# The chain of matrix exponentials moves from a stage of its own into the first attention: the Taylor rounds into its fill, the squarings and products into its drain

## The chip, the cores and the metric

One Trainium2 chip, one of its cores. The metric is the device time of one execution in microseconds (us). Engines: TensorE (PE), VectorE (DVE), ScalarE (ACT), GpSimd (POOL) and SyncE (SP), which issues most transfers.

## The reference

Four layers, each a cross-attention and a feed-forward, on x of 16 x 256 tokens by 128, with 64 context rows per batch. What matters here is in layer 0:

```python
x = x + xattn0(layernorm(x), ctx)            # 16 heads, key mask
# layer 0's feed-forward, on xn = layernorm(...)
moe      = sum over 6 experts of weight * (gelu(xn @ ew1[e] + eb1[e]) @ ew2[e] + eb2[e])
for i in range(4):
    moe  = moe @ expm(gens[i])               # gens: 4 matrices of 128 x 128
abel     = gelu(xn @ aw1 + ab1) @ aw2 + ab2
x        = x + residual + gated mix of abel and moe
```

The four rotations depend on weights alone, so the kernel computes R = expm(g0) expm(g1) expm(g2) expm(g3) once and folds it into the down weights: W2R = ew2 R, b2R = eb2 R. Each exponential is a Taylor polynomial of degree 8 of the matrix scaled by 2^-6, and six squarings.

## The kernel before

The program is a row of stages; a stage ends at a barrier of all engines. The first ones are `load`, `prep_mha` (keys and values), `mha(core, 0, key_mask=True)` (the first attention), `fold_rotations` (the exponentials) and `ffn_moe_rotated`. The feed-forward needs X and its statistics MV from the attention, and W2R, b2R, up_h and up_l from `fold_rotations`.

**The attention** is a software pipeline written out by hand: every engine runs a loop over slots t = -8 to 43 (FIRST = -8, LAST = T + 12, T = 32 tiles of 128 tokens), and an engine's order within a slot is the order of the `if`s in its loop. Slots -8 to -1 are the fill, 32 to 43 the drain. On PE a slot has scores (t), scores_T (t-5), shifts, heads_T (t-10), attend (t-7), tokens (t-9), x_transposes and queries (for four tiles at once, in slots -7, -6 and -3, -2 of the fill, then every four slots) and output (t-10). On DVE: bn_stats and bn_aggr of the second half of x (`arrive`, slots -7, -6, -5 and -3), reciprocal and at (t-10), X (t-11), largest (t), statistics, and q_low after each `queries`. On ACT: attended, normalise, heads_T (the copy aT), exponentials (t-5), shifts, and the copies xT and qh. Queries go out to memory and come back stacked (`write_queries`, `read_queries` on SP) before scores may read them. POOL builds keys(b) (L605), a memset of a part of qs for the first three batches (L632) and add_bo(b) (L609), as far ahead as its buffers go.

**The chain** (`fold_rotations`) works on two halves of two matrices each. A Taylor round: PE multiplies A1T by E (L1085, 4 matmuls), DVE adds A1 from PSUM into tmp (L1124) and scales tmp into the next E (L1125, from SBUF to SBUF); seven rounds, then a transpose (L1090) and its copy (L1128). A squaring: PE makes E E and its transpose (L1097, L1098, 8 matmuls), DVE adds twice the old (L1136, L1137); in the sixth it also adds the identity (L1140, L1141). Then three products (L1103, L1105, L1108) with copies, and the fold (L1111, L1112: 13 matmuls), copied out by L1151 and L1152. A matmul of 32-bit data shows as two entries in the trace. ACT and POOL meanwhile make up_h (L1067) and up_l (L1072). Steps wait on each other by the semaphores s_pe, s_dve, s_r and s_rp.

All weights of later stages, and the mask of the last attention (raw3, 1 MB), are loaded by `load_later` on SP during `prep_mha`.

Of the kernel before, what the change touches and what calls it, by code (L numbers as in the profile page):

```python
# [316 lines left out]

def mha(core, L, mask=None, key_mask=False, gather=False):
# [13 lines left out]
    with Stage(core, f"mha{L}") as st:  # L332
# [95 lines left out]
        def _(pe):  # L428
# [95 lines left out]
        def _(act):  # L524
# [50 lines left out]
            for t in range(FIRST, LAST):  # L575
# [14 lines left out]
                if t % QT == 2 and live(t + 6):  # L590
                    q_evac(quad(t + 6))

        @blk.gpsimd
        def _(pool):
# [32 lines left out]
            else:  # L627
                for b in range(B):
                    keys(b)
                    if key_mask and b < QB:  # L630
                        pool.wait_ge(s["k"], b + 1)
                        pool.memset(qs[b][3 * HR:K0, :, :].bitcast(F32), 1.0).then_inc(s["one"], 1)  # L632
                        pool.wait_ge(s["one"], b + 1)
                    add_bo(b)

        @blk.vector
        def _(dve):
            def pipeline(masked):
# [44 lines left out]
                for t in range(FIRST, LAST):  # L683
# [355 lines left out]
TAYLOR = 8  # L1039
SQUARINGS = 6  # L1040


def fold_rotations(core):


    w = lambda n: core.w("rot", n)
    ident = core.w("ctx", "ident")
    N4 = NROT * P
    with Stage(core, "rot") as st:
        A1, A1T = st.sb("A1", [P, N4]), st.sb("A1T", [P, N4])  # L1050
        E = [st.sb(f"E{u}", [P, N4]) for u in range(2)]
        ET = [st.sb(f"ET{u}", [P, N4]) for u in range(2)]
        tmp, R = st.sb("tmp", [P, N4]), st.sb("R", [P, P])
        MT, M34 = st.sb("MT", [P, P]), st.sb("M34", [P, P])

        pE, pF = ([st.ps(f"p{n}{h}", [P, 512]) for h in range(2)] for n in "EF")
        pW = st.ps("pW", [P, 3, 512])
        pB = st.ps("pB", [P, 512])
        s_pe, s_dve, s_own = ([st.sem(f"{n}{h}") for h in range(2)] for n in ("pe", "dve", "own"))
        s_r, s_rp, s_high = st.sem("r"), st.sem("rp"), st.sem("high")  # L1060
        blk = st.block()
        g = lambda t, n: t[:, P * n:P * n + P]


        @blk.scalar
        def _(act):
            act.activation(core.up_h[:], w("up"), ACT.Copy).then_inc(s_high, 1)  # L1067

        @blk.gpsimd
        def _(pool):  # L1070
            pool.wait_ge(s_high, 1)
            pool.tensor_tensor(core.up_l[:], w("up"), core.up_h[:], ALU.subtract)  # L1072

        W = 2 * P
        half = lambda t, h: t[:, W * h:W * h + W]
        U = (TAYLOR - 1) % 2
        V, VT = (U + SQUARINGS) % 2, SQUARINGS % 2

        @blk.tensor
        def _(pe):  # L1080
            for step in range(TAYLOR - 1):
                for h in range(2):
                    pe.wait_ge(s_dve[h], step + 1)
                    for n in range(2):
                        ins = pe.matmul(g(pE[h], n), g(A1T, 2 * h + n), g(E[step % 2], 2 * h + n), start=True, stop=True)  # L1085
                    ins.then_inc(s_pe[h], 1)
            for h in range(2):
                pe.wait_ge(s_dve[h], TAYLOR)
                for n in range(2):
                    ins = pe.transpose(g(pF[h], n), g(E[U], 2 * h + n), ident)  # L1090
                ins.then_inc(s_pe[h], 1)
            for k in range(SQUARINGS):
                for h in range(2):
                    pe.wait_ge(s_dve[h], TAYLOR + 1 + k)
                    for n in range(2):
                        e, t = g(E[(U + k) % 2], 2 * h + n), g(ET[k % 2], 2 * h + n)
                        pe.matmul(g(pE[h], n), t, e, start=True, stop=True)  # L1097
                        ins = pe.matmul(g(pF[h], n), e, t, start=True, stop=True)  # L1098
                    ins.then_inc(s_pe[h], 1)
            for h in range(2):  # L1100
                pe.wait_ge(s_dve[h], TAYLOR + 1 + SQUARINGS)
                if h == 0:
                    ins = pe.matmul(g(pE[0], 0), g(E[V], 1), g(ET[VT], 0), start=True, stop=True)  # L1103
                else:
                    ins = pe.matmul(g(pE[1], 0), g(ET[VT], 2), g(E[V], 3), start=True, stop=True)  # L1105
                ins.then_inc(s_pe[h], 1)
            pe.wait_ge(s_r, 1)
            pe.matmul(g(pF[0], 0), MT[:], M34[:], start=True, stop=True).then_inc(s_rp, 1)  # L1108
            pe.wait_ge(s_r, 2)
            for c in range(2 * NE):  # L1110
                pe.matmul(pW[:, c // 4, P * (c % 4):P * (c % 4) + P], w("ew2T")[:, P * c:P * c + P], R[:], start=True, stop=True)  # L1111
            pe.matmul(pB[0:NE, 0:P], w("eb2T"), R[:], start=True, stop=True).then_inc(s_rp, 1)  # L1112

        @blk.vector
        def _(dve):
            link = [Chain(dve, s_own[h]) for h in range(2)]
            for h in range(2):
                dve.tensor_scalar(half(A1T, h), half(w("gensT"), h), 2.0 ** -SQUARINGS, None, ALU.mult)
                link[h](dve.tensor_scalar(half(A1, h), half(w("gens"), h), 2.0 ** -SQUARINGS, None, ALU.mult))
                dve.tensor_scalar(half(E[0], h), half(A1, h), 1.0 / TAYLOR, None, ALU.mult).then_inc(s_dve[h], 1)  # L1120
            for step in range(1, TAYLOR):
                for h in range(2):
                    dve.wait_ge(s_pe[h], step)
                    link[h](dve.tensor_tensor(half(tmp, h), pE[h][:, 0:W], half(A1, h), ALU.add))  # L1124
                    dve.tensor_scalar(half(E[step % 2], h), half(tmp, h), 1.0 / (TAYLOR - step), None, ALU.mult).then_inc(s_dve[h], 1)  # L1125
            for h in range(2):
                dve.wait_ge(s_pe[h], TAYLOR)
                dve.tensor_copy(half(ET[0], h), pF[h][:, 0:W]).then_inc(s_dve[h], 1)  # L1128
            i2 = ident.unsqueeze(1).to_broadcast([P, 2, P])
            m2 = lambda t, h: half(t, h).rearrange("p (n d) -> p n d", n=2)  # L1130
            for k in range(SQUARINGS):
                for h in range(2):
                    last = k == SQUARINGS - 1
                    dve.wait_ge(s_pe[h], TAYLOR + 1 + k)
                    dve.wait_ge(s_dve[h], TAYLOR + 1 + k)
# [1449 lines left out]
```

## Time and profile before

| | |
|---|---|
| three runs, us | 1602.37, 1605.2, 1614.73 (median 1605.2) |
| the profiled execution, us | 1620.42, of which 1618.6 are its span |
| mean granted clock of PE in it | 0.828 |
| busy share: PE, DVE, ACT, POOL | 75%, 63%, 38%, 16% |

```profile
## 2 busy tenths in 40 slices
PE   3688769999967655241935885999999999658852
DVE  7577736666647885962337775455566655546768
PEclk9699769999985555565965897999999999968985
```

A slice is 40.5 us; the digits are the busy share in tenths, and PEclk the granted clock of PE in tenths of its full one. In the rows further below, "stretches" give each engine's busy time with its number of instructions, and the timeline gives start, duration, engine, line, operation, output<-inputs, and in brackets the idle time before it with what ended it; PEld is PE's loading of weights. The first attention lies in slices 1 to 4 (31.7 to 170.3 us), the stage of the exponentials in the end of slice 4 and the start of slice 5 (170.6 to 213.7 us), where PE's digit falls.

### The profile page before, as it was taken

What the parts mean: (1) busy time and instruction counts of PE and PEld (TensorE: products, weight loads), DVE (VectorE), ACT (ScalarE), POOL (GpSimd) and SP (SyncE); (2) the same over time, 40 slices, a digit from 0 to 9 for tenths busy, and PEclk for the clock granted to TensorE, in tenths of its full rate; (3) what the DMA queues carried; (4) which work ended last, traced back from release to release, by engine and by line L of the source; (5) the groups of instructions that cost most, each with busy time, mean ns of one, the idle gap of its engine ahead of it and who ended that gap; (6) DMA issues with size and microseconds to landing.
All of it is one profiled execution on the core that took longest, in us unless ns stands there. A gap on an engine that the chain in (4) does not pass through costs nothing. (4 is left out here: it accounts for less than half of the span.)

```text
span 1618.6 us, 22585 instructions
## 1 busy us (share of the span) xinstructions
PE 1213.5 (75%) x6805; PEld 883.7 (55%) x6805; DVE 1012.8 (63%) x3435; ACT 610.2 (38%) x1143; POOL 256.6 (16%) x240
## 2 busy tenths in 40 slices
PE   3688769999967655241935885999999999658852
PEld 1455659898954434210723653677777777425531
DVE  7577736666647885962337775455566655546768
ACT  3565024444433222110223652344443444336641
POOL 1331000010001100043356330000000000023402
PEclk9699769999985555565965897999999999968985
DMA  8441000000000022042215320000000000024301
GB/s 254 127 118 43 1 1 1 1 1 0 1 1 1 0 85 87 1 129 67 87 41 146 95 77 3 0 1 0 1 1 0 0 1 1 1 65 119 99 6 52
DMA packets 57700, 69.43 MB, mean 43 GB/s; under 512 B 10880, under 2 KB 38784, under 8 KB 56960
## 3 DMA queue, kind: packets, MB, share of 16 engines
q1 hardware_dynamic: 54272, 61.78, 13.3%
q0 software_dynamic: 3328, 6.43, 1.3%
q8 instruction: 48, 0.79, 0.2%
q14 instruction: 52, 0.43, 0.1%
HBM read 44.99 MB, written 23.59 MB: 42 GB/s over the span
## 5 line engine op out<-in xcount | busy, mean ns | idle before, releaser
L605 POOL TENSOR_TENSOR mha_ks<-KS,w_ctx 104x1024 fp32r<-104x1024 f32 (+1 forms) x48 | 90.8, 1895 | 674.7 <-POOLq L99 500.0
L2173 DVE SCALAR_TENSOR_TENSOR tree_hl<-tree_pH,tree_hh 128x512 fp32r<-128x512 f32 x192 | 132.4, 690 | 94.5 <-ACT tree_hh L2070 92.5
L2070 ACT ACTIVATE tree_hh<-tree_pH 128x512 fp32r<-128x512 f32 x192 | 114.8, 598 | 146.0 <-PE tree_pH L1974 146.0
L654 DVE TENSOR_REDUCE mha_nm<-mha_pS 128x16 f32<-128x1024 f32 x96 | 117.2, 1221 | 27.4 <-PE mha_pS L449 27.3
L449 PE MATMUL mha_pS<-mha_ks,mha_qs 96*128 96x256 f32 (+1 forms) x384 | 82.6, 344 | 32.6 <-DVE mha_nm L654 18.1
L1323 ACT ACTIVATE ffn_hid<-ffn_pH,w_ffn 128x512 f32<-128x512 f32 x128 | 85.6, 689 | 54.7 <-PE ffn_pH L1248 54.1
L1987 PE MATMUL tree_pY<-tree_hh,w2h 128*128 128x512 f32 x192 | 100.9, 525 | 4.5 <-DVE tree_hl L2173 4.4
L560 ACT ACTIVATE XH<-mha_pST 128x1024 f32<-128x1024 f32 x96 | 98.0, 1021 | 11.8 <-PE mha_pST L470 11.6
L1432 DVE SCALAR_TENSOR_TENSOR ffn_acc<-ffn_pE,ffn_wt,ffn_acc 128x128 f32<-128x128 f32 x192 | 54.1, 346 | 71.3 <-PE ffn_pE L1261 71.3
L1261 PEld LDWEIGHTS ffn_pE<-W2R,ffn_hid 128*128 128x128 f32 x768 | 93.7, 192 | 4.4
L1261 PE MATMUL ffn_pE<-W2R,ffn_hid 128*128 128x128 f32 x768 | 93.9, 276 | 0.0
L449 PEld LDWEIGHTS mha_pS<-mha_ks,mha_qs 96*128 96x128 f32 (+1 forms) x384 | 61.3, 220 | 52.0 <-issue 29.8
L1971 PE MATMUL tree_pH<-tree_xTh,w1h 128*128 128x512 f32 x192 | 81.0, 422 | 1.0 <-DVE tree_sel L2167 1.0
L1973 PE MATMUL tree_pH<-tree_xTh,w1l 128*128 128x512 f32 x192 | 76.5, 398 | 0.0
L1972 PE MATMUL tree_pH<-tree_xTl,w1h 128*128 128x512 f32 x192 | 76.2, 397 | 0.0
L1987 PE MATMUL tree_pY<-tree_hl,w2h 128*128 128x512 f32 x192 | 76.2, 397 | 0.0
L1974 PE MATMUL tree_pH<-tree_sel,mix 128*128 128x512 bf16 x192 | 75.3, 392 | 0.0
L1987 PE MATMUL tree_pY<-tree_hh,w2l 128*128 128x512 f32 x192 | 75.2, 391 | 0.0
L470 PE MATMUL mha_pST<-mha_qs,mha_ks 104*128 104x256 f32 (+1 forms) x384 | 66.2, 297 | 1.9 <-ACT XH L560 0.7
L479 PE MATMUL mha_pO<-XH,VB 128*18 128x256 f32 x768 | 61.1, 390 | 0.0
L433 PE MATMUL mha_pQ<-w_ctx,mha_xh 128*128 128x128 f32 x96 | 20.7, 356 | 51.3 <-ACT mha_xh L535 44.8
L470 PEld LDWEIGHTS mha_pST<-mha_qs,mha_ks 104*128 104x128 f32 (+1 forms) x384 | 55.9, 201 | 4.1 <-ACT XH L560 2.9
(453 smaller groups left out, 2821.8 us busy)
## 6 DMA issues: line engine op xcount, KB each, us to landing
mha_qs<-queries SPq DMA_DIRECT2D x72, 256.0 KB, 4.1
queries<-mha_qh SPq DMA_DIRECT2D x24, 256.0 KB, 2.1
queries<-mha_ql SPq DMA_DIRECT2D x24, 256.0 KB, 2.4
EW<-in_L_W_dram SPq DMA_DIRECT2D x32, 128.0 KB, 2.7
EW<-in_tree_full_dram SPq DMA_DIRECT2D x2, 1536.0 KB, 8.0
slots_in<-route_zero SPq DMA_DIRECT2D x4, 640.0 KB, 10.9
w_rot<-in_rot_dram SPq DMA_DIRECT2D x1, 2307.0 KB, 8.5
X<-in_x_dram SPq DMA_DIRECT2D x8, 256.0 KB, 8.0
```

The costliest lines, as they stand in the source:

```text
L449: ins = pe.matmul(pS[:, NH * g:NH * g + NH, :], qs[u][0:KC, g, c0:c0 + P], ks[b % KB][0:KC, g, :, :], start=True, stop=True)
L470: ins = pe.matmul(pST[:, n, :], ks[b % KB][0:K1, g, h0:h0 + 2, :], qs[u][0:K1, g, c0:c0 + S], start=True, stop=True)
L560: act.activation(PT[b % PB][:, CU * i:CU * i + CU, :], pST[:], ACT.Exp, scale=SC).then_inc(s["P"], 1)
L605: pool.tensor_tensor(ks[b % KB][0:K1, :, :, :], kb, hb, ALU.mult).then_inc(s["k"], 1)
L654: dve.tensor_reduce(nm[:, t, :], pS[:], AX.X, ALU.max, negate=True).then_inc(s["nm"], 1)
L1261: ins = pe.matmul(pE[p % 2][:, j, :], hc, core.W2R[:, P * r:P * r + P], start=(c == 0), stop=(c == 1))
L1323: act.activation(hid[p % 2][:, c, :], pH[c][:], ACT.Gelu, bias=b).then_inc(s["h"], 1)
L1971: pe.matmul(pH[k % 2][:], core.w1h[:, k0], xTh[u][:], start=True, stop=False)
L1973: pe.matmul(pH[k % 2][:], core.w1l[:, k0], xTh[u][:], start=False, stop=False)
L1987: ins = pe.matmul(bank[:], w2[:, k0], h[k % 2][:], start=(c == 0 and i == 0), stop=False)
L2070: act.activation(hh[k % 2][:], pH[k % 2][:], ACT.Relu).then_inc(s["h"], 1)
L2173: dve.scalar_tensor_tensor(hl[k % 2][:], pH[k % 2][:], 0.0, hh[k % 2][:], ALU.max, ALU.subtract).then_inc(s["lo"], 1)
```

## The change

`fold_rotations` is gone. A class `Rotations` has the same steps, numbered k: 0 scales the generators, 1 to 7 are Taylor rounds, 8 the transpose, 9 to 14 the squarings, 15 and 16 the products, 17 the fold. `mha` calls step 0 on DVE ahead of its slots, step k = t + 9 in the fill (t = -8 to -1) and k = t - 23 in the drain (t = 32 to 40). On PE a step stands behind scores and ahead of all else in its slot; on DVE it is last in its slot. Up_h and up_l move to ACT's slot 34 and the end of POOL's work.

The chain has no buffers of its own: E and ET lie in raw3, A1, A1T and tmp in W2R, R and the products in the generators' place; the PSUM is pST in the fill and pS in the drain (the fold also pQ and pST). So the load of raw3 moves from `load_later` into the feed-forward's stage as one transfer, and the generators become a pack of their own (512 KB), loaded on SP between the two halves of x.

```diff
+            rot_at = {t: t + 9 for t in range(-8, 0)}
+            rot_at.update({t: t - T + 9 for t in range(T, T + 9)})
...
                 if live(t):
                     scores(t)
+                if rot and t == UN:
+                    for h in range(2):
+                        pe.wait_ge(rot.s_dve[h], rot.RISING + 1)
+                if t in rot_at:
+                    if t == T:
+                        pe.wait_ge(s["nm"], T)
+                    if rot_at[t] == rot.LAST:
+                        pe.wait_ge(s["P"], TB * B)
+                        pe.wait_ge(s["q"], NG)
+                        pe.wait_ge(core.loaded, 16 * core.loads)
+                    rot.on_tensor(pe, rot_at[t])
                 if live(t - UN):
...
+                if rot and t == T + 2:
+                    act.wait_ge(core.loaded, 16 * core.loads)
+                    act.activation(core.up_h[:], core.w("rot", "up"), ACT.Copy).then_inc(rot.s_high, 1)
...
                     if live(t - HT - 1):
                         dve.wait_ge(s["bn"], x + 1)
                         dve.bn_aggr(MV[:, x, :], bn[x % 2][:])
+                    if t in rot_at:
+                        rot.on_vector(dve, rot_link, rot_at[t])
...
+        @blk.sync
+        def _(sp):
+            sp.dma_start(core.raw3[:], tiles(core.A["mask3"])).then_inc(core.mask3_loaded, 16)
+            sp.wait_ge(core.mask3_loaded, 16)
...
-    for q in range(2):
-        half = slice(T // 2 * q, T // 2 * q + T // 2)
-        later(core.raw3[:, half, :], tiles(A["mask3"])[:, half, :])
...
+                if q == NG // 2 - 1:
+                    sp.dma_start(core.pack["rotg"][:], A["rotg"]).then_inc(core.generators_loaded, 16)
...
-                fold_rotations(core)
```

How PE and DVE take a step in the new code (inside `Rotations`, for each half h, beside the squarings and products, which have the old form):

```diff
+            pe.wait_ge(self.s_dve[h], k)
+            if k < TAYLOR:
+                for n in range(2):
+                    ins = pe.matmul(g(pE, n), g(self.A1T, 2 * h + n), g(E[(k - 1) % 2], 2 * h + n), start=True, stop=True)
...
+            dve.wait_ge(self.s_pe[h], k)
+            if k < TAYLOR:
+                link[h](dve.tensor_tensor(half(self.tmp, h), pE, half(self.A1, h), ALU.add))
+                dve.tensor_scalar(half(E[k % 2], h), half(self.tmp, h), 1.0 / (TAYLOR - k), None, ALU.mult).then_inc(self.s_dve[h], 1)
```

Three places in the engines' order. The first is PE's start of the first attention, before (L433 x_transposes, L438 queries, L449 scores) and after (L555, L560, L571 are the same; L371 a Taylor round of 4 matmuls, L374 the transpose):

```order
L433 MATMUL mha_pQ<-w_ctx,mha_xh 128x128 x4
L438 MATMUL mha_pQ<-mha_xT,w_mha 128x512
L433 MATMUL mha_pQ<-w_ctx,mha_xh 128x128 x4
L438 MATMUL mha_pQ<-mha_xT,w_mha 128x512
L449 MATMUL mha_pS<-mha_ks,mha_qs 128x256 x8
```

```order
L371 MATMUL mha_pST<-raw,W2R 128x128 x8
L555 MATMUL mha_pQ<-w_ctx,mha_xh 128x128 x4
L371 MATMUL mha_pST<-raw,W2R 128x128 x4
L560 MATMUL mha_pQ<-mha_xT,w_mha 128x512
L371 MATMUL mha_pST<-raw,W2R 128x128 x12
L555 MATMUL mha_pQ<-w_ctx,mha_xh 128x128 x4
L371 MATMUL mha_pST<-raw,W2R 128x128 x4
L560 MATMUL mha_pQ<-mha_xT,w_mha 128x512
L374 MATMUL mha_pST<-w_ctx,raw 128x128 x4
L571 MATMUL mha_pS<-mha_ks,mha_qs 128x256 x8
```

Two rounds now stand ahead of the first x_transposes, a third ahead of the first queries, six ahead of the second x_transposes, seven ahead of the second queries, and the whole rising half of the chain ahead of the first scores.

The second is DVE at the same place, after (L872 and L876 statistics of x, L783 q_low, L413 and L414 a half of a round); before, the same rows stood there without L413 and L414:

```order
L413 TENSOR_TENSOR W2R<-mha_pST,W2R 128x256
L414 TENSOR_SCALAR raw<-W2R 128x256
L872 BN_STATS mha_gbn<-X 128x6 x4
L876 BN_AGGR MV<-mha_gbn 128x2 x4
L783 SCALAR_TENSOR_TENSOR mha_ql<-mha_pQ,w_mha,mha_qh 128x512
L413 TENSOR_TENSOR W2R<-mha_pST,W2R 128x256
L414 TENSOR_SCALAR raw<-W2R 128x256
L413 TENSOR_TENSOR W2R<-mha_pST,W2R 128x256
L414 TENSOR_SCALAR raw<-W2R 128x256
```

The third round's adds stand behind q_low, which waits for the queries, which on PE stand behind the third round's matmuls.

The third is DVE in the drain, before (L691 to L716, five operations a slot) and after, in slots 37 and 38, with the sixth squaring between them:

```order
L697 TENSOR_TENSOR mha_at<-mha_pA,mha_rc 128x128
L704 TENSOR_TENSOR X<-mha_pY,X 128x128
L709 BN_STATS mha_bn<-X 128x6
L716 BN_AGGR MV<-mha_bn 128x2
L691 RECIPROCAL mha_rc<-mha_pA 128x16
L697 TENSOR_TENSOR mha_at<-mha_pA,mha_rc 128x128
```

```order
L855 BN_AGGR MV<-mha_bn 128x2
L420 SCALAR_TENSOR_TENSOR raw<-raw,mha_pS 128x256
L421 SCALAR_TENSOR_TENSOR raw<-raw,mha_pS 128x256
L424 TENSOR_TENSOR raw<-raw,w_ctx 128x256
L425 TENSOR_TENSOR raw<-raw,w_ctx 128x256
L420 SCALAR_TENSOR_TENSOR raw<-raw,mha_pS 128x256
L421 SCALAR_TENSOR_TENSOR raw<-raw,mha_pS 128x256
L424 TENSOR_TENSOR raw<-raw,w_ctx 128x256
L425 TENSOR_TENSOR raw<-raw,w_ctx 128x256
L830 RECIPROCAL mha_rc<-mha_pA 128x16
L836 TENSOR_TENSOR mha_at<-mha_pA,mha_rc 128x128
```

Between the statistics of one tile and the reciprocal of the next now stand eight operations of the chain.

## Rows read from the trace of the kernel before

**Rows 1.** Stretches: length; busy PE, PEld, DVE, ACT, POOL; PEclk; DMA share, GB/s.

```profile
37.00:44.00 7.00, 3.39 (x7) 1.45 (x8) 2.93 (x17) 3.67 (x9) 6.64 (x5) 0.50 0.00 0
44.00:51.50 7.50, 2.96 (x6) 0.98 (x5) 2.59 (x15) 2.82 (x6) 5.02 (x5) 0.50 0.79 223
147.50:159.60 12.10, 10.31 (x88) 6.27 (x87) 6.74 (x30) 7.67 (x15) 0.00 (x0) 1.00 0.03 7
159.60:170.60 11.00, 6.60 (x39) 3.74 (x39) 6.34 (x27) 2.10 (x8) 0.00 (x0) 0.79 0.00 0
170.60:182.80 12.20, 8.28 (x32) 7.13 (x32) 9.46 (x20) 1.91 (x1) 3.81 (x1) 0.50 0.01 2
182.80:188.60 5.80, 5.12 (x29) 3.67 (x28) 5.23 (x15) 0.00 (x0) 0.00 (x0) 0.97 0.00 0
188.60:202.00 13.40, 12.39 (x98) 11.18 (x96) 10.26 (x26) 0.00 (x0) 0.00 (x0) 1.00 0.01 1
```

**Rows 2.** Timeline (start us, us, engine, line): the stage of the exponentials, its ends.

```profile
170.12 0.18 DVE L716 BATCH_NORM_AGGREGATE MV<-mha_bn 128x2 f32<-128x6 f32 x1
...
170.60 1.92 ACT L1067 ACTIVATE up_h<-w_rot 128x2048 fp32r<-128x2048 f32 x1 [2.01 <-PEq L99]
...
213.44 0.27 DVE L1152 COPY b2R<-rot_pB 6x128 f32<-6x128 f32 x1
```

**Rows 3.** Timeline: a GpSimd operation and DVE's beside it, at three places.

```profile
33.90 1.80 POOL L632 MEMSET mha_qs<- 3x2048 f32 x1
...
34.86 0.87 DVE L746 TENSOR_SCALAR mha_nt<-mha_nt 128x16 f32<-128x16 f32 x1
...
37.81 1.89 POOL L605 TENSOR_TENSOR mha_ks<-KS,w_ctx 107x1024 fp32r<-107x1024 f32 x1
...
172.59 3.81 POOL L1072 TENSOR_TENSOR up_l<-w_rot,up_h 128x2048 fp32r<-128x2048 f32 x1 [32.80 <-ACTq L99]
...
173.22 3.33 DVE L1125 TENSOR_SCALAR rot_E<-rot_tmp 128x256 f32<-128x256 f32 x1
...
176.91 0.29 DVE L1125 TENSOR_SCALAR rot_E<-rot_tmp 128x256 f32<-128x256 f32 x1
```

**Rows 4.** Timeline: the fill, from the scales to the first scores.

```profile
35.98 0.17 DVE L748 SCALAR_TENSOR_TENSOR mha_NB<-MV,RS 128x16 f32<-128x16 f32 x1
...
36.97 0.38 DVE L735 BATCH_NORM_AGGREGATE MV<-mha_gbn 128x2 f32<-128x6 f32 x4
...
37.98 1.09 PE L433 MATMUL mha_pQ<-w_ctx,mha_xh 128*128 128x128 f32 x4 [7.74 <-ACT mha_xh L535]
...
39.76 2.07 PE L438 MATMUL mha_pQ<-mha_xT,w_mha 128*128 128x512 f32 x2 [0.69 <-ACT mha_xT L540]
...
42.67 0.75 DVE L644 SCALAR_TENSOR_TENSOR mha_ql<-mha_pQ,w_mha,mha_qh 128x512 fp32r<-128x512 f32 x1 [4.00 <-ACT mha_qh L545]
...
48.52 0.64 POOL L609 TENSOR_TENSOR X<-X,w_mha 128x256 f32<-128x256 f32 x1
...
51.55 1.19 PE L449 MATMUL mha_pS<-mha_ks,mha_qs 99*128 99x256 f32 x4 [3.91 <-issue]
```

**Rows 5.** Timeline: the chain's own steps, from a round to the fold.

```profile
178.67 1.78 PEld L1085 LDWEIGHTS rot_pE<-rot_E,rot_A1T 128*128 128x128 f32 x8 [0.28 <-DVE rot_E L1125]
...
180.74 1.78 PEld L1085 LDWEIGHTS rot_pE<-rot_E,rot_A1T 128*128 128x128 f32 x8 [0.28 <-DVE rot_E L1125]
...
203.56 0.42 DVE L1141 TENSOR_TENSOR rot_ET<-rot_ET,w_ctx 128x256 f32<-128x256 f32 x1
...
206.46 4.63 PEld L1111 LDWEIGHTS rot_pW<-rot_R,w_rot 128*128 128x128 f32 x24 [0.68 <-DVE rot_R L1148]
...
211.64 1.89 DVE L1151 COPY W2R<-rot_pW 128x512 f32<-128x512 f32 x3 [5.23 <-PE rot_pB L1112]
```

**Rows 6.** Timeline: the drain, scores_T (L470), heads_T (L492), statistics (L716).

```profile
152.79 0.54 PEld L470 LDWEIGHTS mha_pST<-mha_qs,mha_ks 107*128 107x128 f32 x4 [0.32 <-ACT XH L560]
...
159.66 0.33 PE L492 MATMUL mha_pA<-w_ctx,mha_at 128*128 128x128 f32 x1 [0.52 <-DVE mha_at L697]
...
160.16 0.18 DVE L716 BATCH_NORM_AGGREGATE MV<-mha_bn 128x2 f32<-128x6 f32 x1
...
161.66 0.33 PE L492 MATMUL mha_pA<-w_ctx,mha_at 128*128 128x128 f32 x1 [0.52 <-DVE mha_at L697]
```

More of the change, by code:

```diff
@@ L381, in mha @@
         LD, LM, LW = 16 * 3, 16, 16 * 2
+        if key_mask:
+            rot = Rotations(core, st, pST[:].rearrange("p c s -> p (c s)"), pS[:].rearrange("p h k -> p (h k)"),
+                            pQ[:], pST[:].rearrange("p c s -> p (c s)")[:, 0:512])
+            rot_at = {t: t + 9 for t in range(-8, 0)}
+            rot_at.update({t: t - T + 9 for t in range(T, T + 9)})
+        else:
+            rot, rot_at = None, {}
         blk = st.block()
@@ L505, in _ @@
                     scores(t)
+                if rot and t == UN:
+                    for h in range(2):
+                        pe.wait_ge(rot.s_dve[h], rot.RISING + 1)
[7 more added lines that the diff above has]
+                    rot.on_tensor(pe, rot_at[t])
                 if live(t - UN):
@@ L634, in _ @@
                     add_bo(b)
+            if rot:
+                pool.wait_ge(rot.s_high, 1)
+                pool.tensor_tensor(core.up_l[:], core.w("rot", "up"), core.up_h[:], ALU.subtract)
         @blk.vector
@@ L753, in _ @@
             scales(0)
+            if rot:
+                rot_link = [Chain(dve, rot.s_own[h]) for h in range(2)]
+                rot.on_vector(dve, rot_link, 0)
             if gather:
@@ L1038 @@
 NROT, NE, EH = 4, 6, 256
[L1039 to L1135, printed above, removed]
-                    link[h](dve.scalar_tensor_tensor(half(E[(U + k + 1) % 2], h), half(E[(U + k) % 2], h), 2.0, pE[h][:, 0:W], ALU.mult, ALU.add))
-                    ins = dve.scalar_tensor_tensor(half(ET[(k + 1) % 2], h), half(ET[k % 2], h), 2.0, pF[h][:, 0:W], ALU.mult, ALU.add)
-                    if last:
-                        link[h](ins)
-                        link[h](dve.tensor_tensor(m2(E[V], h), m2(E[V], h), i2, ALU.add))
-                        ins = dve.tensor_tensor(m2(ET[VT], h), m2(ET[VT], h), i2, ALU.add)
-                    ins.then_inc(s_dve[h], 1)
-            dve.wait_ge(s_pe[0], TAYLOR + SQUARINGS + 1)
-            link[0](dve.tensor_copy(MT[:], g(pE[0], 0)))
-            dve.wait_ge(s_pe[1], TAYLOR + SQUARINGS + 1)
-            dve.tensor_copy(M34[:], g(pE[1], 0)).then_inc(s_r, 1)
-            dve.wait_ge(s_rp, 1)
-            dve.tensor_copy(R[:], g(pF[0], 0)).then_inc(s_r, 1)
-            dve.wait_ge(s_rp, 2)
-            for n in range(3):
-                dve.tensor_copy(core.W2R[:, 512 * n:512 * n + 512], pW[:, n, :])
-            dve.tensor_copy(core.b2R[:], pB[0:NE, 0:P])
@@ L2430, in four_layers @@
             with ExitStack() as early:
-                place(core, early, ["mha0", "rot"])
+                place(core, early, ["mha0", "rotg", "rot"])
                 core.itok = sb(early, "itok", [P, B * SK], I32)
@@ L2504, in packs @@
     A = lambda k: np.asarray(I[n + k])
-    out["rot"] = [("gens", A("gens").transpose(1, 0, 2).reshape(P, -1)), ("gensT", A("gens").transpose(2, 0, 1).reshape(P, -1)),
-                  ("ew2T", A("ew2").reshape(-1, P).T), ("eb2T", A("eb2").T),
+    out["rotg"] = [("gens", A("gens").transpose(1, 0, 2).reshape(P, -1)), ("gensT", A("gens").transpose(2, 0, 1).reshape(P, -1))]
+    out["rot"] = [("ew2T", A("ew2").reshape(-1, P).T), ("eb2T", A("eb2").T),
                   ("up", np.concatenate([A("ew1").transpose(1, 0, 2).reshape(P, -1), A("aw1")], 1))]
```

97 lines of the change are left out of this document (added).

## The prediction

> **What bounds the kernel now.** I read the busy time by stretch first [rows 1], since the page's shares are averages over stages. The stage that goes, from the last statistics of the attention at 170.30 us (170.12 + 0.18) to its last copy at 213.71 (213.44 + 0.27), takes 43.4 us in which nothing else runs [rows 2]. It is a chain of PE and DVE handing each other one matrix: in the timeline PE waits for DVE and DVE for PE [rows 5]. So what it gives back, if the work costs nothing elsewhere, is 43.4 us. What it costs elsewhere depends on what the fill and the drain are made of. In the fill PE is busy for 3.39 of 7.0 and 2.96 of 7.5 us, at a granted clock of 0.50, the lower level of 1.2 GHz [rows 1]. That looks like room, but it is a chain too: scales, x_transposes, queries, q_low, memory and back, scores [rows 4]. In the drain PE is busy for 10.31 of 12.1 us up to 159.6, at 1.00, so there is next to no room in slots 32 to 36, and 6.60 of 11.0 us afterwards [rows 1]. POOL is busy for 6.64 of 7.0 us in the first part of the fill and idle in the drain.
>
> **The fill, step by step.** Each round takes 2.07 us with both halves under way at PE's lower clock (178.67 to 180.74) [rows 5]; PE's part is 4 passes of a half in 1.05 us, and 0.1 to 0.2 us pass to the next engine. The scaling operation of DVE, from SBUF to SBUF, is the thing to look at. Alone it took 0.29 us; started at 173.22 beside POOL's up_l it took 3.33 and ended at 176.55, just behind POOL's end at 176.40. So did a smaller one beside a memset: 34.86 + 0.87 = 35.73, POOL's end 35.70 [rows 3]. In the fill POOL works without a break on keys (1.89 us), memset (1.80) and add_bo (0.64) until it has done all it may, at 49.16 before [rows 3, 4]. So each of the first scalings waits for the end of a POOL operation, and two of them a round do so in turn.
>
> From the scales' end at 36.15 [rows 4]: step 0 is six operations, done at 38.2. Round 1: PE's half 0 at 38.2, half 1 at 39.4; the scalings end with keys(1) at 40.2 and with the second memset at 42.1. Round 2 on PE ends at 43.3, and only then come the first x_transposes, 5.3 us later than before (37.98). On DVE a pass of statistics takes 1.3 us (it ended 36.97 + 0.38 = 37.35, behind the scales' end) [rows 4], and round 2's scalings end with keys(2) and the third memset at 44.9 and 46.8. Round 3 on PE ends at 48.0, then queries (before 39.76, so +8.2), and q_low ends 3.66 us behind its start (39.76 to 43.42), at 51.7. Before, 8.1 us of memory traffic followed (43.42 to 51.55) and set the first scores. Now these run beside the rest of the chain, which lasts longer: round 3 on DVE until 54.9 (keys(3) and add_bo stand in its way), statistics 1.3, round 4 until 57.7, round 5 60.0, statistics again, round 6 62.8; on PE x_transposes and round 7 until 64.3; queries to q_low 3.66, until 68.0; round 7 on DVE 69.5; the transpose 70.0; first scores. Against 51.55 that is 18.5 us. PE is busy almost without a gap from 57 on; in the old stage its clock rose from 0.50 to 0.97 in the stretch behind a like one, 8.28 busy of 12.2 us [rows 1], so I take 1.0 us off for the second queries: **+17.5**. Everything behind the first scores shifts by that: the four later tiles' queries are back before their scores want them, and SP, ACT and POOL have nothing else to be late with. What is late next is nothing new.
>
> The ends for the fill: if scalings did not wait for POOL, the same list gives 13.6, 12.6 with the clock; if also the six of step 0 and the rest waited, 20.5. I take the row, since the operation is the same one, of the same size, beside the same engine.
>
> **The drain.** A squaring is 16 passes, 11.18 / 6 = 1.86 us of weight loads at full clock [rows 1]. PE has it ahead of scores_T in slots 32 to 36, where it idled for some 0.3 us a slot waiting for the exponentials (0.32 at 152.79) [rows 6]: 5 x (1.86 - 0.3) and a little more in slot 32, **+8.1**. DVE has some 1.3 us of its own in a slot (27 operations in 6.34 us [rows 1], five a slot, and gaps) and now four of 0.42 (203.56 [rows 5]), 1.8 with gaps, which fits into a PE slot of 3.6. In slot 37 the sixth squaring has eight such operations, 3.5 us with gaps, which start behind the statistics (160.34 + 8.1 = 168.4) and end at 171.9; the next tile's heads_T, before at 161.66 [rows 6], needs DVE's reciprocal and product first and comes at 172.6: +10.9 so far, **+2.8** for this. Steps 15 and 16 are three small copies and three matmuls, hidden but for **0.2** in a loop of 2.0 us between PE, DVE and ACT (159.66 to 161.66). The fold is 13 matmuls, 26 passes, 5.2 us (206.46 to 211.64), then copies of 2.07 us (211.64 to 213.71) [rows 2, 5]; of these 7.3, 2.4 lie beside the loop of the tiles 30 and 31: **+4.9**. I take the lower clock for the fold, since before it fell at the end of the drain (0.79 over its last stretch [rows 1]); at the full one it is 2.2 less. Up_h is 1.92 us on ACT [rows 2], which is busy for 7.67 us of five and a half slots [rows 1], 1.4 of now 3.6 each: **+0.4**; up_l is on an idle POOL, and no DVE operation of the drain at that time is a scaling. Together **+16.4**; low end 13.4 (fold at full clock, nothing for up_h, no loss in the sixth squaring's hand-over), high end 18.
>
> **The rest at nothing.** The mask's load now runs in the feed-forward's stage, where SP has nothing and the data is wanted four stages later. The generators' load stands on SP's queue ahead of the second half of x, which is first read at 36 us. The stage's barrier (0.3 us) is the same one fewer on both sides of my sum's ends.
>
> **The sum.** 43.4 - 17.5 - 16.4 = 9.5 us less. On the profiled execution, 1620.4 us, that gives 1610.9. This execution stands 15.2 us above the median of the three runs, and the difference carries over: 1605.2 - 9.5 = **1595.7**. Best and worst of the bounds: 43.4 - 12.6 - 13.4 = 17.4 and 43.4 - 20.5 - 18 = 4.9 less, so 1588 to 1600; the three runs lie 2.8 below and 9.5 above their median, which widens it to **1585 to 1604**.
>
> **Rivals.**
> 1. *The fill hides its part.* If the memory traffic behind q_low went on setting the first scores, the delay would be that of the first q_low alone, 8.2 us or, without waits on POOL, 4.8. Then the saving is 43.4 - 16.4 - 8.2 = 18.8 and up to 22: 1583 to 1586. For it speaks that the fill's PE is half idle. Against it: rounds 4 to 7 follow one another behind q_low in both queues, and 5 rounds of 2 us and two passes of statistics are more than 8.1. 10%.
> 2. *PE falls to its lower clock in the drain* (the case on the other side). Its place is slots 32 to 37: PE now waits for DVE at each step. At 1.2 GHz six squarings cost 11.2 us more and the attention's own matmuls of five slots, about 1.7 us each, 8.5 more: 43.4 - 17.5 - 36.1, a loss of 10: 1615. It decides against the change once half of this comes. Against it: before, PE kept 1.00 through 159.6 at 10.31 busy of 12.1 us, and kept it into the sparser part; the new slots are denser. By the Trainium skill, "TensorE: Matmul & The Clock Gate", section "HAM oscillation — how this bites in real kernels", short bursts of matmuls with waits between them bring the array back to half its clock again and again. If that page's rule held for the handing to and fro in these slots, the time would be this rival's; the rows of the drain before do not show it. 6%.
> 3. *DVE and POOL block each other more than counted*, also POOL for DVE, so that keys(3) and later keys come late and the first slots stall: another 5 us, a saving of 4.5: 1600.7. Within my range. 12%.
> 4. *The start of the first slots gets the full clock* after the dense fill (before 0.50): five slots at 0.4 us each, saving 11.5: 1593.7, within my range too.
>
> **Chances.** The forecast with rivals 3 and 4 has 80%, rival 1 10%, rival 2 6%, the rest 4%. Measurement of this kernel tells about 1%, 16 us, from no change. Faster by over 1%, below 1589.2, needs a saving of 16: rival 1, and the better end of mine, together 22%. Slower by over 1%, above 1621: 3%. Within 1%: 75%.
>
> **What would show it.** Right: first scores at about 69 us, first x_transposes at 43; several scalings (L414) of 1 to 2 us which end with a POOL operation; slots of the drain 3.6 us apart; the sixth squaring's eight DVE operations just ahead of a reciprocal, and PE idle there; the end of the attention at some 204 us, against 213.7 of the old stage. Wrong: first scores near 60 (rival 1), a granted clock below 0.9 in the first part of the drain (rival 2), or scalings of 0.29 us throughout.

## The result, and the profile after

| | before | after |
|---|---|---|
| median of 6 runs each, us | 1607.52 (1602.37 to 1614.73) | 1594.61 (1591.95 to 1597.61) |
| ratio, 95% interval | | 0.9919 (0.9892 to 0.9946) |
| the profiled execution, us | 1620.42 | 1597.43, of which 1595.6 are its span |
| mean granted clock of PE in it | 0.828 | 0.833 |

The change gives 12.9 us, between 8.7 and 17.4. The forecast was 1595.7 and the measurement 1594.6, but so close a hit is partly luck: the saving forecast was 9.5, and the median of before came out 2.3 us higher than in the three runs it was taken from.

The page of the changed kernel, its second part (slices of 39.9 us):

```profile
PE   4688879999957664244916885999999999658852
...
PEclk9699979999975555565955997999999999969985
```

Counted from slice 0, the first attention and the chain now end with slice 4, and PE's digits in slices 4 and 5, before 7 and 6, are 8 and 7.

Stretches of the changed kernel (length; busy PE, PEld, DVE, ACT, POOL; PEclk; DMA share, GB/s), in the form of [rows 1]: the drain with the squarings, a stretch behind them, the fold, the feed-forward's stage and the routing's:

```profile
161.70:185.50 23.80, 21.96 (x202) 17.85 (x200) 18.49 (x63) 10.18 (x17) 3.81 (x1) 1.00 0.02 6
...
188.50:190.00 1.50, 1.04 (x5) 0.91 (x5) 0.70 (x4) 0.28 (x1) 0.00 (x0) 0.50 0.00 0
190.00:193.50 3.50, 3.50 (x29) 3.16 (x27) 1.05 (x5) 0.00 (x0) 0.00 (x0) 0.90 0.00 0
...
198.30:454.20 255.90, 235.39 (x1600) 212.53 (x1601) 154.62 (x703) 108.07 (x173) 20.29 (x16) 0.95 0.02 5
454.20:739.30 285.10, 142.54 (x478) 94.89 (x478) 203.14 (x969) 64.27 (x124) 43.40 (x48) 0.54 0.14 47
```

The timeline of the changed kernel in the fill, to be read beside [rows 3] and [rows 4] (L889 is the last of the scales, L371 and L374 are PE's Taylor rounds and transpose, L413 and L414 DVE's add and scaling, L741 and L768 POOL's keys and memset, L783 q_low, L571 the first scores):

```profile
35.95 0.17 DVE L889 SCALAR_TENSOR_TENSOR mha_NB<-MV,RS 128x16 f32<-128x16 f32 x1
...
39.78 1.83 POOL L768 MEMSET mha_qs<- 3x2048 f32 x1
...
40.24 1.53 DVE L414 TENSOR_SCALAR raw<-W2R 128x256 f32<-128x256 f32 x1
...
42.84 1.06 PE L555 MATMUL mha_pQ<-w_ctx,mha_xh 128*128 128x128 f32 x4
...
47.30 1.91 PE L560 MATMUL mha_pQ<-mha_xT,w_mha 128*128 128x512 f32 x2
...
50.05 0.75 DVE L783 SCALAR_TENSOR_TENSOR mha_ql<-mha_pQ,w_mha,mha_qh 128x512 fp32r<-128x512 f32 x1 [2.63 <-ACT mha_qh L678]
...
51.05 1.89 POOL L741 TENSOR_TENSOR mha_ks<-KS,w_ctx 107x1024 fp32r<-107x1024 f32 x1
...
51.16 1.93 DVE L414 TENSOR_SCALAR raw<-W2R 128x256 f32<-128x256 f32 x1
...
53.46 0.30 DVE L414 TENSOR_SCALAR raw<-W2R 128x256 f32<-128x256 f32 x1
...
55.44 0.29 DVE L414 TENSOR_SCALAR raw<-W2R 128x256 f32<-128x256 f32 x1
...
61.90 1.02 PE L560 MATMUL mha_pQ<-mha_xT,w_mha 128*128 128x512 f32 x2
...
63.68 0.75 DVE L783 SCALAR_TENSOR_TENSOR mha_ql<-mha_pQ,w_mha,mha_qh 128x512 fp32r<-128x512 f32 x1 [2.39 <-ACT mha_qh L678]
...
66.00 0.71 PE L571 MATMUL mha_pS<-mha_ks,mha_qs 99*128 99x256 f32 x4
```

The scaling that starts at 40.24 ends at 41.77, right behind the memset's end at 41.61; the one at 51.16 ends at 53.09, behind the keys' end at 52.94. With no POOL operation beside it one takes 0.29 (at 55.44). The first scores come at 66.00, 14.45 us later than in [rows 4].

The same in the drain, beside [rows 6] (L379 the squarings, L614 heads_T, L384 the first of the products' steps, L359 the fold, L392 its copies, L855 statistics):

```profile
159.60 0.72 PE L571 MATMUL mha_pS<-mha_ks,mha_qs 99*128 99x256 f32 x4
...
173.63 0.39 PE L379 MATMUL mha_pS<-raw 128*128 128x128 f32 x2
...
177.26 0.39 PE L379 MATMUL mha_pS<-raw 128*128 128x128 f32 x2
...
179.53 0.27 PE L614 MATMUL mha_pA<-w_ctx,mha_at 128*128 128x128 f32 x1
...
185.61 0.49 PE L384 MATMUL mha_pS<-raw 128*128 128x128 f32 x2 [1.22 <-DVE raw L425]
186.18 0.33 PE L614 MATMUL mha_pA<-w_ctx,mha_at 128*128 128x128 f32 x1
...
190.01 2.28 PE L359 MATMUL mha_pS<-w_rotg,w_rot 128*128 128x128 f32 x16
...
193.54 1.29 DVE L392 COPY W2R<-mha_pS 128x512 f32<-128x512 f32 x2 [2.32 <-PE mha_pST L360]
...
196.22 0.33 PE L614 MATMUL mha_pA<-w_ctx,mha_at 128*128 128x128 f32 x1 [1.37 <-DVE mha_at L836]
...
198.10 0.18 DVE L855 BATCH_NORM_AGGREGATE MV<-mha_bn 128x2 f32<-128x6 f32 x1
```

The row of the kernel before that scores(31) is counted from:

```profile
145.05 0.72 PE L449 MATMUL mha_pS<-mha_ks,mha_qs 99*128 99x256 f32 x4
```

Slots are 3.6 us apart (173.63 to 177.26), and the attention ends at 198.28, where the old stage ended at 213.71 [rows 2]: 15.4 us earlier in the trace. It splits into 43.4 saved, 14.45 paid in the fill and 13.4 in the drain (scores(31), at 159.60, to the end took 38.68 us, before 25.25). Between the first scores and scores(31) nothing changed: 93.6 us, before 93.5.

### The profile page after: what moved, and what is told of

The parts are those of the page before. It is cut to its first block and busy times, and to the rows that moved or that the text cites. A ratio compares the mean times of both kernels' runs of the same rounds, so it can differ in the third digit from the quotient of the medians.

```text
span 1595.6 us, 22581 instructions
## 1 busy us (share of the span) xinstructions
PE 1206.2 (76%) x6805; PEld 880.0 (55%) x6805; DVE 1014.6 (64%) x3435; ACT 608.7 (38%) x1143; POOL 255.4 (16%) x240
## 3 DMA queue, kind: packets, MB, share of 16 engines
q1 hardware_dynamic: 51328, 61.78, 13.4%
## 5 line engine op out<-in xcount | busy, mean ns | idle before, releaser
L741 POOL TENSOR_TENSOR mha_ks<-KS,w_ctx 104x1024 fp32r<-104x1024 f32 (+1 forms) x48 | 90.8, 1894 | 686.8 <-POOLq L99 498.0
L2208 DVE SCALAR_TENSOR_TENSOR tree_hl<-tree_pH,tree_hh 128x512 fp32r<-128x512 f32 x192 | 132.3, 689 | 93.9 <-ACT tree_hh L2105 92.0
L571 PE MATMUL mha_pS<-mha_ks,mha_qs 96*128 96x256 f32 (+1 forms) x384 | 81.6, 340 | 25.9 <-DVE mha_nm L793 21.6
L1296 PE MATMUL ffn_pE<-W2R,ffn_hid 128*128 128x128 f32 x768 | 93.5, 275 | 0.0
L571 PEld LDWEIGHTS mha_pS<-mha_ks,mha_qs 96*128 96x128 f32 (+1 forms) x384 | 59.9, 215 | 44.0 <-issue 22.7
L1281 PE MATMUL ffn_pH<-ffn_xTh,up_h 128*128 128x512 f32 x128 | 57.2, 447 | 0.8 <-ACT ffn_hid L1358 0.5
```

The source lines that it names most:

```text
L571: ins = pe.matmul(pS[:, NH * g:NH * g + NH, :], qs[u][0:KC, g, c0:c0 + P], ks[b % KB][0:KC, g, :, :], start=True, stop=True)
L741: pool.tensor_tensor(ks[b % KB][0:K1, :, :, :], kb, hb, ALU.mult).then_inc(s["k"], 1)
L1296: ins = pe.matmul(pE[p % 2][:, j, :], hc, core.W2R[:, P * r:P * r + P], start=(c == 0), stop=(c == 1))
L2208: dve.scalar_tensor_tensor(hl[k % 2][:], pH[k % 2][:], 0.0, hh[k % 2][:], ALU.max, ALU.subtract).then_inc(s["lo"], 1)
```

## The experiments

Seven variants of the changed kernel were timed and profiled, and the kernel before was profiled a second time; all ratios are to the kernel before. The first attention does not start at the same time in every profile: the last of the scales starts at 35.95 us in the changed kernel's and between 35.16 and 35.84 in those of the variants without a stage ahead. Counted from there the four profiles with the same fill agree on the first scores within 0.02 us (30.04 to 30.06), so differences in the fill are best counted from there too.

**Fill alone, drain alone.** The two halves of the change, one at a time. In `fill_only` the rising half stays in the fill and the falling half has its own stage behind the attention; in `drain_only` the rising half has its own stage ahead of the attention. The cores of the two diffs:

```diff
             rot_at = {t: t + 9 for t in range(-8, 0)}
-            rot_at.update({t: t - T + 9 for t in range(T, T + 9)})
...
                 mha(core, 0, key_mask=True)
+                falling_stage(core)
```

```diff
-            rot_at = {t: t + 9 for t in range(-8, 0)}
-            rot_at.update({t: t - T + 9 for t in range(T, T + 9)})
+            rot_at = {t: t - T + 9 for t in range(T, T + 9)}
...
                 prep_mha(core, 0, True, statistics=True)
+                rising_stage(core)
```

> The Taylor rounds and the transpose stay in the fill of the first attention; the squarings, products and the fold go back into a stage of their own behind it, with up_h and up_l. My theory (fill and drain each cost what their own chains say, and add up): the first scores stay at 66 us, the drain is as in the kernel before, so the attention ends at about 185, and the stage takes 25 (before: 188.6 to 213.7). Less than before by 43.4 - 25.1 - 14.5 = 4 us, ratio 0.9975. The rival (the fill hides the rising half and the drain carries the whole cost) wants some 18 us less than before, ratio 0.989.

> The rising half (scaling, Taylor rounds, transpose) gets a stage of its own ahead of the first attention; the falling half stays in the drain. My theory: that stage takes 15 us (18 in the kernel before, of which 3 was one scaling waiting for POOL, which is idle here), the fill is as before (first scores 15.5 us behind the stage's start, so as late as now), the drain costs 13.4. Less than before by 43.4 - 15.3 - 13.4 = 14.7 us, ratio 0.991, the same as with the rounds in the fill: the fill's placement by itself gives nothing. The rival (the fill's room hides a good part of the rounds) wants this kernel to be 10 us slower than the changed one, ratio 0.997.

Measured: `fill_only` 1606.92 us, ratio 1.0007 (0.9990 to 1.0025); `drain_only` 1594.51, ratio 0.9920 (0.9898 to 0.9941), which is the changed kernel's own. The rival of `drain_only` (0.997) falls, and so does that of `fill_only` (0.989). The timeline of `drain_only`, where the chain's rounds are done before the first x_transposes (L572; L588 the scores):

```profile
52.42 1.09 PE L572 MATMUL mha_pQ<-w_ctx,mha_xh 128*128 128x128 f32 x4 [7.00 <-ACT mha_xh L685]
...
65.99 1.19 PE L588 MATMUL mha_pS<-mha_ks,mha_qs 99*128 99x256 f32 x4 [3.91 <-issue]
```

65.99 against 66.00: in the fill the rising half costs what it costs in a stage of its own ahead of it, and the placement in the fill gives nothing. Of the some 15.5 us in the trace, 11.7 are the falling half's (25.1 in the old stage, 13.4 in the drain). The other 3.8 are the rising half's, 18.3 in the old stage and 14.5 in either of the new places; 3.0 of them are the one scaling that up_l held up in the old stage (3.33 against 0.29 us [rows 3]). Starting up_l elsewhere in the kernel before would have shown whether these 3.0 can be had without moving anything; it wasn't tried.

`fill_only` was to bring 4 us, since the rising half had taken 18.3 in the old stage (170.3 to 188.6) and delays the first scores by 14.5. Its profile shows what took most of them back. Stretches, of the start of its falling stage and of the one ahead of it:

```profile
183.00:185.20 2.20, 0.80 (x2) 0.50 (x2) 0.94 (x4) 0.19 (x2) 0.00 (x0) 0.50 0.00 0
185.20:189.40 4.20, 3.79 (x18) 3.83 (x19) 0.84 (x2) 1.85 (x1) 2.27 (x1) 0.50 0.00 0
```

The stage takes 27.4 us where the same steps took 25.1 in the old stage (188.6 to 213.7). There the clock stood at 0.97 in the stretch ahead of the squarings [rows 1]; here it had already fallen at the sparse end of the drain (0.50 in the 2.2 us ahead of the stage, with PE busy for 0.80), and the squarings stay at 0.50 for the stage's first 4.2 us. By the starts of the rows, 1.3 of the 2.3 us lie in the squarings and products (19.1 us against 17.8), 0.7 in the fold up to its copies (5.85 against 5.18), and 0.3 ahead of the first squaring. The fold's part need not be the split's: its 24 entries took 4.83 us in the first profile of the kernel before and 5.46 in the second. The saving left in the trace is 1.1 us; the time shows none, and its interval allows up to 1.6.

**Do the scalings wait for POOL?** `tmp_psum` writes the round's sum back to PSUM in place, so that the scaling reads PSUM instead of SBUF; nothing else changes.

```diff
-                link[h](dve.tensor_tensor(half(self.tmp, h), pE, half(self.A1, h), ALU.add))
-                dve.tensor_scalar(half(E[k % 2], h), half(self.tmp, h), 1.0 / (TAYLOR - k), None, ALU.mult).then_inc(self.s_dve[h], 1)
+                link[h](dve.tensor_tensor(pE, pE, half(self.A1, h), ALU.add))
+                dve.tensor_scalar(half(E[k % 2], h), pE, 1.0 / (TAYLOR - k), None, ALU.mult).then_inc(self.s_dve[h], 1)
```

> The changed kernel with one edit: a round's sum is written back to PSUM in its place instead of to tmp in SBUF, so the scaling that follows reads PSUM. My theory (the scaling from SBUF to SBUF waits for POOL's operation): the scalings take 0.42 us each without exception, first scores 3 us earlier, at 63, and the attention ends at 195.3; ratio to before 0.990. The rival (DVE's waits are hidden behind queries and transposes anyway): scalings of 0.42 but first scores at 66 and no gain.

Measured: 1592.57 us, ratio 0.9920 (0.9903 to 0.9937). Its timeline:

```profile
36.99 1.94 POOL L741 TENSOR_TENSOR mha_ks<-KS,w_ctx 107x1024 fp32r<-107x1024 f32 x1
37.91 0.42 DVE L414 TENSOR_SCALAR raw<-mha_pST 128x256 f32<-128x256 f32 x1
...
60.61 1.20 PE L571 MATMUL mha_pS<-mha_ks,mha_qs 99*128 99x256 f32 x4
```

Every scaling takes 0.42, beside POOL or not, and the first scores come at 60.61, 5.4 us earlier; counted from the scales, which started at 35.16 here, it is 4.6. The five scalings that were held up in the changed kernel (1.17, 1.53, 0.89, 1.53 and 1.93 us) had lost 5.6 us over 0.29 each, and 14 scalings at 0.42 cost 1.8 more, which leaves 3.8; the first queries also took 1.02 us instead of 1.91. The theory of the lock is shown, and the rival (hidden waits) falls. The Trainium skill, "SBUF — State Buffer", section "Who interferes with whom", says that scalar-and-tensor operations of VectorE from SBUF may take ports that it shares with GpSimd, and that the later one then waits for the whole instruction: the pair of profiles agrees, 1.53 against 0.42. The attention's end came 4.2 us earlier in the trace, counted from the scales. The time does not show it: 2 us by the medians and nothing by the ratios (0.9920 against 0.9919, intervals of 3 to 5 thousandths), so how much of the 4.2 arrives is not settled by this run.

**Does the order in PE's queue set the fill's price?** `late_rounds` takes a slot's round behind its x_transposes and queries instead of ahead of them.

```diff
-                if t in rot_at:
+                if t in rot_at and t >= 0:
...
                     queries(quad(t + 6))
+                if t in rot_at and t < 0:
+                    rot.on_tensor(pe, rot_at[t])
```

> The changed kernel with one edit: in the fill PE takes a slot's round behind x_transposes and queries instead of ahead of them. My theory (in the changed kernel the queries stand in line behind rounds that wait for DVE, and the rounds behind the queries' way through ACT and DVE, so the two chains add up): first x_transposes at 38, the first q_low 2 us earlier, the second transposes and queries beside rounds 6 and 7; first scores at 60 instead of 66, the attention ends at 192, ratio to before 0.988. The rival (the rounds' own chain sets the first scores): no more than 2 us.

Measured: 1587.22 us, ratio 0.9884 (0.9867 to 0.9900). Its timeline:

```profile
38.42 1.06 PE L555 MATMUL mha_pQ<-w_ctx,mha_xh 128*128 128x128 f32 x4
...
42.22 1.92 PE L560 MATMUL mha_pQ<-mha_xT,w_mha 128*128 128x512 f32 x2
...
59.70 0.72 PE L571 MATMUL mha_pS<-mha_ks,mha_qs 99*128 99x256 f32 x4
```

The work is the same, and the first scores come 6.3 us earlier than in the changed kernel; x_transposes come 4.4 and the queries 5.1 us earlier. The scales started at 35.33, 0.6 earlier than there, so 5.7 of the fill's 14.5 us were due to the order alone. The rival (no more than 2 us) falls. The attention's end came 6.9 us earlier, counted from the scales, and by the ratios the time is 5.6 us shorter.

**What is a squaring worth in the drain?** `three_squarings` leaves out three of the six.

```diff
-SQUARINGS = 6
+SQUARINGS = 3
...
-            rot_at.update({t: t - T + 9 for t in range(T, T + 9)})
+            rot_at.update({t: t - T + 9 for t in range(T, T + rot.LAST - rot.RISING)})
```

> The changed kernel without three of the six squarings in the drain (the slots for the products and the fold come three slots earlier); the generators are still scaled by 2^-6, so the rotations that come out are other ones. The fill is the same. Theory (each squaring in slots 32 to 36 adds its own passes on PE, 1.8 us less the 0.3 us PE idled there, and the last squaring and the fold cost what they did): three slots shorter by 1.5 us each, the attention's end at about 193.8 us instead of 198.3; ratio to the kernel before 0.989. Rival (the drain's price is all in the last squaring's eight DVE operations and in the fold; the squarings before them lie beside work that DVE or ACT sets anyway): the end moves by 1 us or less, 197.3, and the ratio stays 0.992. A further one: with the fold in a denser slot (37), nothing of it lies behind the last tiles, and the end comes another 2 to 3 us earlier, at 191.

Measured: 1591.51 us, ratio 0.9893 (0.9876 to 0.9911). The first scores came at 65.56 and the last statistics ended at 193.64:

```profile
65.56 0.72 PE L571 MATMUL mha_pS<-mha_ks,mha_qs 99*128 99x256 f32 x4
...
193.46 0.18 DVE L855 BATCH_NORM_AGGREGATE MV<-mha_bn 128x2 f32<-128x6 f32 x1
```

That is 128.1 us between them, 132.3 with all six: 1.4 us for each squaring, if the steps behind them cost the same. The rival that they lie beside other work falls, and the further one too, since the end did not come at 191.

**Do the fold's copies hold up the last tile?** `fold_act` gives the four copies to ACT, one slot later.

```diff
+                if rot and t == T + 9:
+                    rot.on_scalar(act)
...
         if k == self.LAST:
-            dve.wait_ge(self.s_rp, 2)
-            for n in range(2):
-                dve.tensor_copy(self.core.W2R[:, 512 * n:512 * n + 512], self.falling[:, 512 * n:512 * n + 512])
```

> The changed kernel with one edit: the four copies that take the fold's results out of PSUM are ACT's, one slot later, instead of DVE's. Theory (they stand in DVE's queue between the fold and the last tile's heads, which wait 1.4 us for DVE's product of heads): the last heads_T no longer waits, and the attention's end comes 1 to 2 us earlier, at 196.3 to 197.3 us; ratio to the kernel before 0.991, which this many rounds do not tell from 0.992. Rival (ACT's copies, 4 x 0.6 us, end as late as DVE's did and stand in ACT's way to the last tile): the end at 198.3 or later.

Measured: 1591.79 us, ratio 0.9901 (0.9884 to 0.9917). Its timeline from the fold on:

```profile
190.40 3.52 PE L359 MATMUL mha_pS<-w_rotg,w_rot 128*128 128x128 f32 x16
...
195.06 0.33 PE L616 MATMUL mha_pA<-w_ctx,mha_at 128*128 128x128 f32 x1
...
197.00 0.33 PE L616 MATMUL mha_pA<-w_ctx,mha_at 128*128 128x128 f32 x1 [0.53 <-DVE mha_at L840]
...
198.88 0.18 DVE L859 BATCH_NORM_AGGREGATE MV<-mha_bn 128x2 f32<-128x6 f32 x1
```

The two heads_T are 1.94 us apart instead of 2.79, so the edit takes away 0.85. But the attention ended at 199.06, later than 198.28, because in this execution the fold's first 16 entries took 3.52 us instead of 2.28. The stretch 190.00 to 195.00 was granted 0.63. By the end alone the rival was right, and the time tells neither; two kernels whose fold's first 16 entries took 1.95 us each do (`combined` follows below). From the fold's start to the attention's end `late_rounds`, with DVE's copies, took 8.24 us (182.53 to 190.77), and `combined`, with ACT's, 7.08 (180.10 to 187.18). The copies on ACT save 1.2 us, as the theory had it, though the last of them ends 0.17 us behind the attention's own end.

**All three edits together.** `combined` is `late_rounds`, `tmp_psum` and `fold_act` in one.

> Three edits of the changed kernel at once: PE takes a slot's round of the rising half behind that slot's x_transposes and queries, the sum of a round goes back to PSUM so that the scaling reads PSUM, and the fold's copies are ACT's. Theory (the rising half in the fill is one more chain in the same in-order queues, and its length beside the queries is what delays the first scores; the saving adds up): first scores at 56 to 57.5 us (66.0 in the changed kernel, 60.6 and 59.7 with one of the first two edits alone), end of the attention at about 187 to 188 us instead of 198.3, ratio to the kernel before 0.986. Rival (the two fill edits remove the same delay, or the last Taylor round behind the second queries sets the start whatever stands ahead): first scores not below 59, end at 190 or later, ratio 0.988 as with the later rounds alone.

Measured: 1584.98 us, ratio 0.9863 (0.9846 to 0.9879), faster than both kernels. Timeline and stretches:

```profile
56.58 0.72 PE L573 MATMUL mha_pS<-mha_ks,mha_qs 99*128 99x256 f32 x4
...
180.10 1.95 PE L359 MATMUL mha_pS<-w_rotg,w_rot 128*128 128x128 f32 x16
...
187.00 0.18 DVE L861 BATCH_NORM_AGGREGATE MV<-mha_bn 128x2 f32<-128x6 f32 x1
```

```profile
37.00:44.00 7.00, 6.17 (x29) 5.11 (x27) 6.30 (x26) 2.71 (x7) 6.80 (x6) 0.67 0.00 0
44.00:51.50 7.50, 4.84 (x24) 4.25 (x25) 6.80 (x24) 0.65 (x3) 4.34 (x4) 0.80 0.64 176
51.50:57.00 5.50, 4.19 (x23) 2.76 (x23) 5.06 (x17) 2.31 (x6) 0.00 (x0) 0.96 0.26 97
```

The first scores come at 56.58, 5.0 us behind the old ones, and the attention ends at 187.18. Counted from the scales, which started at 35.20 here, the savings at the first scores are 5.7 and 4.6 alone and 8.7 together, of 10.3, so most of them adds up and the rival falls; 5.8 us of the fill's price are left. DVE is busy for 18.2 of these 20.0 us, so its own work is the likely limit; this is argued and not shown. Giving some scalings to ACT would be the test; it wasn't made.

**What scatters behind the first attention?** In the first profile the routing's stage is 8 us longer before than after, which the change does not touch. A second profile of the unchanged kernel:

> The kernel before, unchanged, for a second profile of it. Theory (the first profile's stage of routing was some 8 us longer by the run, not by the kernel): the routing stage, from the first ptop_pk to the first exp_pX, takes 285 us as in the changed kernels, not 293, while the first attention ends at the same times as in the first profile, within 0.5 us. Rival (the old placement makes the routing itself longer, so the change saves there too): 293 us again.

The row of the routing's stage in the first profile of before:

```profile
470.00:763.40 293.40, 140.37 (x478) 94.25 (x478) 202.91 (x969) 64.28 (x124) 43.12 (x48) 0.55 0.14 46
```

and in the second:

```profile
466.70:750.90 284.20, 139.84 (x478) 94.26 (x479) 203.09 (x969) 64.05 (x124) 43.86 (x48) 0.55 0.14 47
```

284.2 us against 285.1 in the changed kernel: the 293 belonged to that one execution. The attention agreed within 0.5 us between the two profiles (the chain's stage ended at 213.22 and 213.71). From there to the end of the span this second profile took 1392 us, the changed kernel's 1397, and the profiles of the others between 1392 and 1402, without any relation to their edits. The first profile of before took 1405. So the time behind the attention scatters by some 10 us from execution to execution, and a difference of a few us is read from the trace up to the attention's end, and from medians.

## Why the prediction was right, and where it was off

**The saving of the stage, 43.4.** Nothing came in its place, and the three phases measured (43.4 - 14.45 - 13.4) give 15.5, the trace 15.4.

**The fill, +17.5 forecast, 14.45 measured.** The mechanism was as told: x_transposes at 42.84 (43.3 forecast), the first queries at 47.30 (48.0), q_low's end at 50.80 (51.7), the memory traffic hidden by the rest of the chain. The lead grew along it. It was 0.9 by q_low and 1.1 when round 3 ended on DVE (53.76, not 54.9), because the second scaling started when add_bo had only 0.13 us left and was not held up. Rounds 4 to 6 went nearly as listed, a round in 2.07 at a granted clock of 0.50, and ended at 61.29 instead of 62.8, a lead of 1.5. Then PE did x_transposes and round 7 in 2.2 us (59.72 to 61.90), at 0.71 and in part beside round 6 on DVE, and reached the second queries at 61.90 instead of 64.3: 2.4. The queries themselves took 1.02 instead of 2.07, so that q_low ended 2.5 us behind their start, not 3.7: 3.6. Round 7 on DVE and the transpose brought the lead to 4.0, of which the sum had taken off 1.0 for the clock. So the term that was too large is the list of times, by 3.0 us together: 1.1 in the first three rounds, and most of the rest from x_transposes and round 7 on, which the list laid behind DVE's round 6 and at the lower clock.

**The drain, +16.4 forecast, 13.4 measured**, by the starts of heads_T counted from scores(31):

| term | forecast | measured |
|---|---|---|
| five squarings (and up_h) | 8.1 + 0.4 | 7.3 |
| the sixth squaring with its eight operations | 2.8 | 2.7 |
| the products | 0.2 | 0.0 |
| fold and its copies | 4.9 | 3.45 |

A squaring added 1.45 us a slot in the changed kernel (7.3 / 5) and 1.40 in `three_squarings`, where the sum had 1.86 - 0.3 = 1.56. In the sixth, PE idled 1.22 us for DVE, as told. The fold was taken at the lower clock, 5.2 us; it took 3.5 at 0.90. The forecast named 2.2 us less for the full clock, and the row fell between. The first 16 entries took 1.95, 1.95, 1.99, 2.05, 2.12, 2.28 and 3.52 us in the seven profiles that have the fold in the drain: the step of the prediction that failed most here is taking the lower clock for it, which came near only in one of the seven (`fold_act`).

**The sum.** Both terms were too large by 3.0, so the trace's saving was 15.4 instead of 9.5; it lies inside the bounds 4.9 to 17.4 that were worked out. The time measured lies between, at 12.9. The range stated was narrower than its own working: 1600.3 and 9.5 above it make 1610, not 1604. Steps chosen on the cautious side (a lock for each scaling, the lower clock) all erred the same way, and adding them up doubled the miss. The chances stood on it: a saving of 16 us was the bound for faster by over 1%, and the trace came within 0.6 of it.

**The rivals.** The first (the fill hides its part) is refuted for this kernel by the first scores at 66.00 and by `drain_only`; reordering, as in `late_rounds`, brings 5.7 us of it. The second (the lower clock in the drain) did not come: 21.96 busy of 23.8 us at 1.00 with all of PE's waits for DVE in it. Behind these slots it fell, to 0.50 from 188.50 to 190.00, with PE busy for 1.04 of 1.5 us; this is the clock that the fold began with. The section of the Trainium skill that spoke for it ("TensorE: Matmul & The Clock Gate", "HAM oscillation — how this bites in real kernels") describes waits between short bursts; the waits of these slots, 1.22 us and less in the rows read, did not bring what it describes, and no run here lengthened them. The third (more blocking) did not come: five scalings were held up, one less than forecast, and POOL was not late for any slot; its own operations beside them took up to 0.05 us longer (keys 1.94 us instead of 1.89). The fourth (the first slots at full clock) gave nothing: the first scores took 0.71 instead of 1.19 us, but the distance to scores(31) stayed, since the next scores waited for DVE's largest of the last ones all the same.

**Work costed at nothing.** The mask's load moved into the feed-forward's stage, which took 255.9 us, before 256.3 and 253.5 in its two profiles, so no price of it can be seen.

## What to carry to other kernels

In this kernel a chain of small dependent steps was cheap beside a phase whose engine is busy with independent work: a squaring of 1.86 us of passes cost 1.4 there. Beside another dependent chain it cost what a stage of its own would (14.5 us), unless PE's queue took the urgent chain's step first. Ask of every slot which of the two steps someone far away waits for, and put that one ahead: two lines moved brought 5.6 us by the ratios, the placement in the fill by itself nothing. When VectorE scales SBUF to SBUF while GpSimd works, count up to GpSimd's operation length for it (0.89 to 3.33 us here for 0.29), or read from PSUM (0.42). And split the saving of a move by what was moved: 3.0 us of this one are a wait for GpSimd that stood in the old stage, and not a gain of the new place.

## What the runs showed of the hardware

- DVE's scaling of 128x256 from SBUF took 0.29 us alone and 0.89 to 1.93 beside POOL in the changed kernel (3.33 in the one before), ending 0.15 to 0.16 us behind POOL's operation each time, also where this was a memset that reads nothing; from PSUM it took 0.42 in both cases. The add in front of it, PSUM and SBUF, took 0.41 beside POOL as alone.
- PE's clock fell in the sparse ends of the drain, ahead of a barrier: in `fill_only` 0.50 over the last 2.2 us with PE busy for 0.80, and the stage behind started at 0.50 and kept it for 4.2 us. This cost 1.3 us in the squarings and products.
- The fold's first 16 entries, the same matmuls at the same place of the drain, took 1.95 to 2.28 us in six profiles and 3.52 in one.
